# Maxima in triples, twelve units of the second phase moved into the product stage, and another order of the first tiles

## The reference

```python
residual = hidden_states                                  # (4, 2048, 640)
enc, ca = ctx[:, :150, :], ctx[:, 150:, :]                # 150 context rows, 4 tokens, 384 wide
hs = _mha(hidden_states @ Wq, enc @ Wk, enc @ Wv)         # 8 heads of 80
ca_q1 = jnp.einsum('btc,th->bch', ca, Wq_ca)              # (4, 384, 640)
ca_q1 = ca_q1[:, indices, :]                              # 384 rows repeated to 2048 by linspace
ca_hs1 = _mha(ca_q1, residual, residual)                  # attention of those over all 2048 rows of x
ca_hs2 = _mha(ca_hs1 @ Wq, ca @ Wk_ca, ca @ Wv_ca)        # four keys per head
out = (hs + ca_hs2) @ Wout + b_out + residual
```

## Time and profile before

| what | value |
|---|---|
| median of 3 runs | 1661.28 us (1656.25 to 1666.82) |
| the profiled execution | 1659.01 us |
| its span | 1657.2 us |
| TensorE busy | 1576.5 us, 95% of the span |
| VectorE busy | 808.4 us, 49% |
| ScalarE busy | 626.5 us, 38% |
| chain that ended last, by engine | TensorE 86%, VectorE 6%, ScalarE 5% |
| mean granted TensorE clock | 0.959 of full |

### The profile page before, as it was taken

How to read it: one execution, slowest core, us unless ns; L and a number is a source line. 1 busy time by engine, 2 the same in 40 slices (tenths; PEclk the granted TensorE clock), 3 DMA queues, 4 the chain that set the end, 5 groups by cost and what they waited for, 6 DMA issues and landing times.

```text
span 1657.2 us, 24648 instructions
## 1 busy us (share of the span) xinstructions
PE 1576.5 (95%) x10294; PEld 1268.5 (77%) x10294; DVE 808.4 (49%) x1623; ACT 626.5 (38%) x1314; POOL 2.8 (0%) x12
## 2 busy tenths in 40 slices
PE   6999899999999989999999998999999999899999
PEld 4853489999884369998987337999998634899998
DVE  5567345344457543544446745344344672544533
ACT  1426524223243742322333374233233256332322
POOL 0000000000000000000000000000000000000000
PEclk9999899999997899999999799999999979999999
DMA  6530002120252001122026000113004400021101
GB/s 224 185 132 13 5 21 92 51 106 25 96 189 77 1 7 51 61 73 82 32 97 220 37 1 11 48 61 145 18 33 153 161 33 1 18 80 53 64 17 40
DMA packets 46648, 116.47 MB, mean 70 GB/s; under 512 B 3645, under 2 KB 5301, under 8 KB 45003
## 3 DMA queue, kind: packets, MB, share of 16 engines
q1 hardware_dynamic: 37036, 93.91, 16.2%
q10 hardware_dynamic: 9503, 21.00, 3.2%
HBM read 76.53 MB, written 38.37 MB: 69 GB/s over the span
## 4 chain that ended last, share of the span: by engine, by line
PE 86%; DVE 6%; ACT 5%; issue 2%; DMA 0%; SPq 0%; ACTq 0%; DVEq 0%
PE ps_w L483 44%; PE ps_s L483 17%; PE ps_t L483 15%; PE ps_t L493 9%; DVE unit_max L1198 3%; ACT work L1028 2%; DVE ot L1362 1%; ACT ot L1056 1%; ACT work L1009 0%; PE ps_s L493 0%; DMA y_all<-in_L_xattn_Wv_ca_dram 0%; PE ps_w L493 0%; ACT work L936 0%; DVE neg_max L1245 0%; ACT y_all L943 0%
## 5 line engine op out<-in xcount | busy, mean ns | idle before, releaser
L483 PE MATMUL ps_w<-wo_h,ot 128*128 128x320 f32 x1280 | 327.7, 321 | 1.0 <-DVE ot L1362 1.0
L1198 DVE TENSOR_REDUCE unit_max<-ps_s 128x1 f32<-128x512 f32 x384 | 244.2, 685 | 86.0 <-PE ps_s L483 83.4
L483 PEld LDWEIGHTS ps_w<-wo_h,ot 128*128 128x128 f32 x1280 | 222.0, 188 | 2.0 <-DVE ot L1362 2.0
L483 PE MATMUL ps_w<-wo_l,ot 128*128 128x320 f32 x640 | 197.3, 308 | 0.0
L483 PEld LDWEIGHTS ps_w<-v_all,work 120*128 120x128 f32 x1280 | 177.2, 198 | 9.3 <-issue 9.3
L483 PE MATMUL ps_w<-v_all,work 120*128 120x162 f32 (+1 forms) x1280 | 178.7, 296 | 0.0
L1009 ACT ACTIVATE work<-ps_s,neg_max 128x150 f32<-128x150 f32 x512 | 155.0, 394 | 44.8 <-DVE neg_max L1249 44.8
L493 PE MATMUL ps_t<-ident,work 128*120 128x128 f32 (+1 forms) x960 | 140.2, 277 | 8.7 <-ACT work L993 4.5
L993 ACT ACTIVATE work<-ps_t 120x512 f32<-120x512 f32 (+1 forms) x128 | 62.9, 491 | 212.2 <-PE ps_t L493 212.2
L483 PE MATMUL ps_s<-keys_h,qt_h 128*128 128x300 f32 (+1 forms) x448 | 134.2, 299 | 0.0
L483 PE MATMUL ps_s<-keys_h,qt_l 128*128 128x300 f32 (+1 forms) x448 | 131.5, 294 | 0.0
(11 more groups left out here) (157 smaller groups left out, 2294.9 us busy)
## 6 DMA issues: line engine op xcount, KB each, us to landing
xc<-in_x_dram SPq DMA_DIRECT2D x32, 1280.0 KB, 6.6
out_dram<-work ACTq DMA_DIRECT2D x64, 320.0 KB, 2.2
xt_all<-work SPq DMA_DIRECT2D x60, 256.0 KB, 2.4
xt_l<-xt_all SPq DMA_DIRECT2D x12, 1280.0 KB, 5.5
y_all<-in_L_xattn_Wk_dram SPq DMA_DIRECT2D x4, 960.0 KB
y_all<-in_L_xattn_Wv_dram SPq DMA_DIRECT2D x4, 960.0 KB
pick<-in_pick_dram SPq DMA_DIRECT2D x16, 194.0 KB
xc<-in_L_xattn_Wq_dram SPq DMA_DIRECT2D x1, 1600.0 KB, 10.7
```

Of the source, the lines that this page charges most:

```text
L483: return nc.tensor.matmul(out, lhs, rhs, start=start, stop=stop, skip_group_check=True)
L1198: v.tensor_reduce(unit_max[:, n, q:q + 1], bank, AX_X, ALU.max).then_inc(max_free, 1)
```

## The change

- **Units in triples.** Every group of units is now three, one per bank, and stands at one of three places of a product step: after `turn_x`, after `products`, or after the queries (`TRIPLES`). Steps 8 to 20 hold 16 triples; four more stand in the tail with five query matmuls between them. Before, groups of two and three alternated, and the tail had single units with two query matmuls between them.
- **Twelve units of phase 1 come early.** Six of chunk 0 and six of chunk 1 stand in the product stage, behind the units of phase 0 of that chunk. The early list so has 60 units and the phase 0 loop 36: two before it, three in each of steps 0 to 10, one in step 11.
- **VectorE's list follows**: 12 units, `split_g`, three, `q0_lows`, three; `q0_lows(3)` moves behind `place_maxima(0)`.
- **Phase 0 loop.** `tile_scores(0)` of bank 0 stands behind step 12, `turn_ca(1)` and bank 1 behind step 13.
- **Phase 1 loop.** The eight exponentials of tile 0's weights stand one by one in steps 1 to 8; `turn_z(0)` behind step 10 instead of 7.
- **First tiles.** `p2`'s exponential, the shares and `pick_window(0)` move behind tile 0's weights and normalisation; `gather(0)` moves from tile 0 into tile 1; `tile_scores(2)` moves from ahead of tile 1's `turn_weights` to behind tile 0's `values`, ahead of `turn_o(0)`; `gather(c+1)` moves to the third tile of a chunk (`GATHER_AT = 2`).

```diff
             order += [("q", c + 1, j) for j in range(KT)]
-        order += [("p", s, part) for part in range(3)]
-        if s == 0:
+        order += [("p", s, part) for part in range(2)]
+        if s == 1:
             order.append(("gather", 0))
+        order.append(("p", s, 2))
         if ahead:
             if t == GATHER_AT:
...
-GATHER_AT = 1
+GATHER_AT = 2
...
-def unit_steps():
-
...
-UNITS_AHEAD, UNITS_AFTER, TAIL = unit_steps()
-UNITS_BEFORE_SPLIT, UNITS_BEFORE_LOW = 7, 10
-Q0_FILL = [0] * 8 + [4, 4, 4, 3, 0, 4, 4, 4, 3, 0, 4, 4, 4]
-Q0_TAIL, Q0_CHAIN = 2, 3
+UNITS_EARLY = 6
+
+
+def unit_order():
+
+    early, late = [], []
+    for q in range(CHUNKS):
+        units = [(ct, r) for ct in range(CT) for r in range(GROUPS)]
+        early += [(0, q, ct, r) for ct, r in units]
+        n = UNITS_EARLY if q + 2 < CHUNKS else 0
+        early += [(1, q, ct, r) for ct, r in units[:n]]
+        late += [(1, q, ct, r) for ct, r in units[n:]]
+    return early + late, len(early)
+
+
+UNIT_ORDER, PHASE0_UNITS = unit_order()
+AFTER_TURNED, AFTER_PRODUCTS, AFTER_QUERIES = range(3)
+TRIPLES = {8: (AFTER_TURNED, AFTER_QUERIES), 9: (AFTER_PRODUCTS,), 10: (AFTER_TURNED,), 11: (AFTER_TURNED,), 12: (AFTER_TURNED,),
...
+UNITS_BEFORE_SPLIT, UNITS_BEFORE_LOW = 12, 15
+Q0_FILL = [0] * 8 + [4, 4, 4, 3, 0, 4, 4, 4, 3, 0, 2, 2, 2]
+Q0_SPLIT, Q0_TURNED, Q0_TRIPLE = 9, 3, 5
+UNITS_STEP = 3
...
-                done = 0
+                done, first = 0, 0
                 for m in range(GX + 1):
...
-                    max_units(*UNITS_AHEAD[m])
+
+                    def triple(place):
+                        nonlocal first
+                        if place in TRIPLES.get(m, ()):
+                            max_units(first, M_BANKS)
+                            first += M_BANKS
+
+                    triple(AFTER_TURNED)
                     if m >= 1:
                         i, kt = divmod(m - 1, KT)
                         products(i, kt)
                         if i and kt == 1:
                             turn_g(i - 1)
-                    max_units(*UNITS_AFTER[m])
+                    triple(AFTER_PRODUCTS)
                     queries0(done, Q0_FILL[m])
                     done += Q0_FILL[m]
-                for u in range(TAIL, UNITS):
-                    n = Q0_MM * 3 - done if u == TAIL else Q0_TAIL if KT * Q0_MM - done > 3 * Q0_CHAIN else 0
-                    queries0(done, n)
-                    done += n
-                    max_unit(u)
-                    if u == TAIL + 2:
-                        turn_g(CHUNKS - 1)
-                queries0(done, Q0_CHAIN)
+                    triple(AFTER_QUERIES)
+                queries0(done, Q0_SPLIT)
+                turn_g(CHUNKS - 1)
+                done += Q0_SPLIT
+                queries0(done, Q0_TURNED)
+                done += Q0_TURNED
+                for u in range(first, PHASE0_UNITS, M_BANKS):
+                    max_units(u, M_BANKS)
+                    if u + M_BANKS < PHASE0_UNITS:
+                        queries0(done, Q0_TRIPLE)
+                        done += Q0_TRIPLE
...
+                queries0(done, 2 * Q0_TRIPLE)
                 turn_ca(0)
-                queries0(done + Q0_CHAIN, KT * Q0_MM)
-                max_units(UNITS, 2)
+                queries0(done + 2 * Q0_TRIPLE, KT * Q0_MM)
+                max_units(PHASE0_UNITS, 2)
                 scores(0, 0)
+                first = PHASE0_UNITS + 2
                 for st in range(NST):
                     if st + 1 < NST:
                         scores(0, st + 1)
-                    max_units(UNITS + 2 + 3 * st, 3 if st + 1 < NST else 1)
+                    units = min(UNITS_STEP, PHASES * UNITS - first)
+                    max_units(first, units)
+                    first += units
                     weigh(0, st)
-                tile_scores(0, (0,))
-                turn_ca(1)
-                tile_scores(0, (1,))
+                    if st == 12:
+                        tile_scores(0, (0,))
+                    if st == 13:
+                        turn_ca(1)
+                        tile_scores(0, (1,))
                 scores(1, 0)
                 tile_scores(0, (2,))
                 for st in range(NST):
                     if st + 1 < NST:
                         scores(1, st + 1)
                     weigh(1, st)
-                    if st == 7:
+                    if st == 10:
                         turn_z(0)
...
-                        tile_scores(s + 1)
+                        if s > 1:
+                            tile_scores(s + 1)
                     turn_weights(s, (0, 1))
+                    if s == 1:
+                        gather(0)
                     if s:
                         project(s - 1, 0)
                     turn_weights(s, (2,))
-                    if s == 0:
-                        gather(0)
                     if c + 1 < CHUNKS and t == GATHER_AT:
                         gather(c + 1)
                     values(s)
+                    if s == 0:
+                        tile_scores(2)
                     if s:
                         project(s - 1, 1, range(0, 2))
                     turn_o(s)
...
+                def weight(s, h):
+                    bank, c = h // 3, h % 3
+                    return nc.scalar.activation(probs[:, h * KEYS:(h + 1) * KEYS], ps_s[:, bank, c * KEYS:(c + 1) * KEYS], exp,
+                                                bias=neg_max[:, s % 2, h:h + 1], scale=SCALE)
+
                 def weights(s):
-                    if s:
-                        use = ("p", s - 1, 1)
-                        act.wait_ge(t_full[bank_of(use)], filled(b, use))
+                    use = ("p", s - 1, 1)
+                    act.wait_ge(t_full[bank_of(use)], filled(b, use))
+                    if s == 1:
+                        remaining_weights(s - 1)
                     act.wait_ge(nmax_ready, tile0 + s + 1)
                     for h in range(HEADS):
-                        if s and (h + 1) * KEYS > 2 * GRP * KR >= h * KEYS:
+                        if s > 1 and (h + 1) * KEYS > 2 * GRP * KR >= h * KEYS:
                             remaining_weights(s - 1)
...
+                        last = weight(s, h)
                     last.then_inc(p_ready, 1)
...
-                        if a and st == 3:
-                            weights(0)
+                        if a and 1 <= st <= HEADS:
+                            if st == 1:
+                                act.wait_ge(nmax_ready, tile0 + 1)
+                            last = weight(0, st - 1)
+                            if st == HEADS:
+                                last.then_inc(p_ready, 1)
...
+                first = 0
                 for i in range(1, CHUNKS):
-                    first = (i - 1) * per_chunk
+                    chunk = per_chunk + (UNITS_EARLY if i < CHUNKS - 1 else 0)
                     unit_maxima(first, UNITS_BEFORE_SPLIT)
                     split_g(i)
-                    unit_maxima(first + UNITS_BEFORE_SPLIT, UNITS_BEFORE_LOW - UNITS_BEFORE_SPLIT)
-                    q0_lows(i - 1)
-                    unit_maxima(first + UNITS_BEFORE_LOW, per_chunk - UNITS_BEFORE_LOW)
+                    if i < CHUNKS - 1:
+                        unit_maxima(first + UNITS_BEFORE_SPLIT, UNITS_BEFORE_LOW - UNITS_BEFORE_SPLIT)
+                        q0_lows(i - 1)
+                        unit_maxima(first + UNITS_BEFORE_LOW, chunk - UNITS_BEFORE_LOW)
+                    first += chunk
                 splits.close()
-                unit_maxima(UNITS - per_chunk, UNITS_BEFORE_SPLIT)
+                q0_lows(2)
+                unit_maxima(first, per_chunk)
+                place_maxima(0)
                 q0_lows(3)
-                unit_maxima(UNITS - per_chunk + UNITS_BEFORE_SPLIT, per_chunk - UNITS_BEFORE_SPLIT)
-                place_maxima(0)
+                take_ca(0)
                 q0_lows(4)
-                unit_maxima(UNITS, UNITS)
+                unit_maxima(PHASE0_UNITS, PHASES * UNITS - PHASE0_UNITS)
                 place_maxima(1)
+                take_ca(1)
                 maxima.close()
...
-                    if s and s + 1 < SLOTS:
+                    if 1 < s < SLOTS - 1:
                         maximum(s + 1)
                     if c + 1 < CHUNKS and t == GATHER_AT:
                         pick_window(c + 1)
-                    turned_weights(s)
+                    if s:
+                        turned_weights(s)
+                    if s == 1:
+                        picked(0)
                     if s:
                         add_rows(s - 1, 0)
-                    if s == 0:
-                        picked(0)
                     if c + 1 < CHUNKS and t == GATHER_AT:
                         picked(c + 1)
                     normalise(s)
+                    if s == 0:
+                        dve.wait_ge(e2_ready, b + 1)
...
+                        pick_window(0)
```

(43 more changed lines are left out.)

38 lines of the change are left out of this document (9 added, 29 removed).

## The result

| | before | changed |
|---|---|---|
| median of 20 runs | 1661.56 us | 1647.32 us (1641.78 to 1666.21) |
| ratio, 95% interval | | 0.9924 (0.9900 to 0.9949) |
| profiled execution, its span | 1659.0, 1657.2 us | 1648.0, 1646.2 us |
| mean granted clock | 0.959 | 0.965 |

The change wins 0.8%, less than half of the forecast of 2.0%, though inside the range of 1608 to 1650.

A forecast was written before the change was run, and what follows sets the result against it. TensorE, busy 95% of the span, was taken as the bound. Gains 0.3 + 4.0 + 3.6 + 0.6 = 8.5 us per element, 34 in all, gave 1625 profiled, 1627.5 as median; range 1608 to 1650.

The forecast's parts named there:

- product stage and tail: Stages ahead of phase 0: fewer groups minus 6.0 us, queries plus 0.7, waits plus 4.9; gain taken as 0.3 per element.
- The walk: Unit-by-unit pass through TensorE's and VectorE's lists with traced durations; for the kernel before it gave 53.8 us, trace 53.7.
- rival 3: New waits drop the product stage's clock: 25 us of half clock per element, 50 us lost in all, 1678 us; chance 0.06.
- signs of being wrong: Product stage clock under 1.00, phase 1 steps of 1.8 us, or the wait for `ot` gone or doubled.
- up to 0.5: Product stage and tail: loss per microsecond of half clock, since the stage has no slack; phase 0 lost 0.26.
- Rival 2: VectorE late in product stage: 2 us more there, phase 1 hides nothing, 18.6 us in all, 1643 us; chance 0.20.
- Phase 0 and middle: From `turn_ca(0)` to phase 1: 38.6 us with 10 us of half clock kept, gain 4.0 per element, bounds 1.5 and 6.6.
- Phase 1: Phase 1 loop with exponentials spread over eight steps: 26.5 us against a mean near 30.1, gain 3.6 per element.
- First tiles: Stretch to tile 1's values: a 3.4 us TensorE wait, gain 0.6 us per element, bounds minus 1 and plus 2.9.
- Main loop, gathers: Gathers and their VectorE work moved to the third tile of a chunk: no TensorE wait, zero gain or loss.
- The Trainium skill's rule: Small idle gaps between matmul groups cycling through PSUM banks toggle the clock; by it, product-stage waits of 0.3 to 1.4 us would.

The follow-up runs named there:

- short reductions: Changed kernel with the first 60 unit reductions reading 256 of 512 columns, TensorE's list untouched: 1610.6 us, ratio 0.9693 to the kernel before.
- the waits put into the kernel before: Kernel before plus four small unused VectorE reductions behind each of the first two query tiles' subtractions: 1698.0 us, ratio 1.0210.
- the last experiment: Kernel with subtraction behind 18 reductions, scores back and triples moved, plus tile 0's scores and second turning behind the phase 0 loop again: 1608.7 us, ratio 0.9663.
- two comparisons of medians: New first-tile order against old: 1648.5 against 1646.6 us on the kernel before with phase 1 spread; 1630.5 against 1630.7 on the changed kernel with subtraction behind 18.
- the kernel with the scores back: Changed kernel with the subtraction behind 18 reductions and tile 2's scores put back behind tile 0's turned output: 1611.0 us, ratio 0.9686.

## Why the prediction was wrong

**The step that failed** is the one on product stage and tail: "Net minus 0.4 us; I take 0.3." It measured plus 7.0 us per element, 28 in all; the forecast missed by 20 us on the medians, 23 on the profiled execution, less than 28 because the other terms came out a little better. Two things were wrong in it. The walk left out the waits of 0.34 us for `g` at the first triple of each chunk, 1 us per element. And it charged the waits at their own length, at the full clock. Their length was about right: 1.0 us at steps 13 and 18 where 1.4 were forecast, 0.6 at steps 9 and 14. The mechanism that filled the gap was written down as rival 3, with a chance of 0.06, and its mark stood under the signs of being wrong: new waits drop the clock in the product stage. The short reductions and the waits put into the kernel before show it from both sides.

**Its price**: 56.3 us with 3.4 us of half clock in product stage and tail (first element), 64.8 with 23.9 (second). That is 0.42 us per microsecond of half clock; "up to 0.5" was right. The four elements have 14.5 us on average, the kernel before 2.1, all of it in the tail; the 12.4 us more are worth 5.2. By the same price, an estimate, the stage would take 54.8 us at the full clock and took 52.8 before: 2.0 us more, where 0.3 less were forecast. One of these 2.3 us is the forgotten waits; the rest of the walk's error is not traced. Rival 3 was sized for 25 us in each element and came at 12.4 more, hence a smaller gain and not a loss. Rival 2 had its 2 us in this stage, but phase 1 hid its work. That the result lies inside the range of 1608 to 1650 is luck: rival 3 as sized gave 1678.

**Phase 0 and middle**: right. 38.5 us in the first element with 10.2 us of half clock, forecast 38.6 with 10. Over the four elements the half clock in it fell from 15.0 us to 7.7 and the gain is 4.6 us, forecast 4.0. One piece was wrong and small: 0.5 us of the scores were to hide in the loop; the last experiment shows 0.1.

**Phase 1**: right. 26.6 us against a forecast of 26.5, a step of 1.65 with an exponential in it against 1.68, no half clock. Alone it is worth 15 us, where four times 3.6 were forecast; the traces give 3.6 on average, with and without the rest of the change.

**First tiles**: mechanism and waits right, the choice wrong. Forecast a wait of 3.4 us for `ot`, measured 3.15; forecast gain 0.6, measured 1.4 in the trace and none in two comparisons of medians, inside the bounds either way. The prediction doubted whether tile 2's scores are better ahead of `turn_o(0)`; the experiment shows that without this one move the stretch gains 3.7 us more.

**Main loop, gathers**: right, nothing moved there; TensorE stands idle for 2.0 us in all ahead of the sixteen gathers of the changed kernel.

**The Trainium skill's rule** on small gaps between groups that cycle through PSUM banks (TensorE: Matmul & The Clock Gate, "A second HAM failure mode: psum-queue depth-cycling") was the better guide. The traces agree, but not in every element: 0.77 and 0.86 in two product stages with the waits and 1.00 in two, 1.00 in all four with the short reductions. The prediction named the rule and saw it borne out by the tail's clock of 0.95, and yet put nothing for it into the sum.

## What to carry to other kernels

A wait of a microsecond in a stage that has run without gaps must be priced twice: once at its length, and once as a possible fall of the clock behind it, here up to 17 us at 0.4 us each. Before a stage is filled up, look at what stands ahead on the engine that frees its buffers: the cure for most of the loss was one number, a subtraction that waits for a third engine moved behind three reductions. And when an order hides one wait, ask what the moved work hid where it was; here it had covered 3 us.

## What was not expected of the hardware

- The half clock outlived its cause. In the second element TensorE was busy for 18.6 of 19.0 us at a mean clock of 0.60:

```profile
476.00:495.00 19.00, 18.56 (x73) 13.70 (x73) 11.32 (x21) 3.50 (x7) 0.00 (x0) 0.60 0.36 126
```

  The same instructions keep 1.00 with the short reductions, where the triple ahead of them takes 0.62 us and not 1.43. So behind the same wait of 1.3 us (0.34 and 1.0) came 17.1 us of half clock in the second element, 10.3 in the third and none in the first and fourth. Why it stayed so long with TensorE busy, no run here settles.
- It did not fall in every element: the same waits left the first and fourth product stage at 1.00. The spread of the runs is wide for the changed kernel, 24 us over 20 runs, and 4 us (1609.0 to 1612.7) over 5 for the kernel with the scores back; in both the slower runs show the lower mean clock.
- Three matmuls of 12 rows each on different row groups take 0.43 us to the next instruction together, and one alone takes the same 0.43 (100.39 to 100.82 in the kernel before); in these lists TensorE pays for the count of groups, not of units.
